# Windowed attention and top-1 experts: whole queries against masked keys in the first scores

## The reference

```python
q = (x @ wq.T + bq); k = (x @ wk.T + bk); v = (x @ wv.T + bv)      # by head, D = 16
loc = einsum('bnihd,bnjhd->bnihj', qw, kw) * D**-0.5               # in windows of 128
gsc = einsum('bihd,bjhd->bihj', q[:, ::32], k[:, ::32]) * D**-0.5  # global tokens, added
attn = softmax(scores, axis=-1)                                    # over all 2048 keys
x = layernorm(x + attn @ v @ wo.T + bo)
h = gelu((layernorm(x) * s_e + b_e) @ W1_e + b1_e); out = h @ W2_e + b2_e
x = layernorm(x + out of the expert argmax(x @ Wg.T))
```

## Time and profile before

| | us |
|---|---|
| median of 3 runs | 445.81 |
| lowest, highest | 444.01, 446.04 |
| profiled execution, span from first to last instruction | 442.8 |

### The profile page before, as it was taken

How to read it: one execution, slowest core, us unless ns; L and a number is a source line. 1 busy time by engine, 2 the same in 40 slices (tenths; PEclk the granted TensorE clock), 3 DMA queues, 4 the chain that set the end, 5 groups by cost and what they waited for, 6 DMA issues and landing times.

```text
span 442.8 us, 14658 instructions
## 1 busy us (share of the span) xinstructions
PE 405.3 (92%) x5747; PEld 339.8 (77%) x5747; DVE 326.1 (74%) x796; ACT 250.6 (57%) x523; POOL 220.4 (50%) x301
## 2 busy tenths in 40 slices
PE   5899799999999999999999899988798998999991
PEld 4758678888888888888888778756577887777891
DVE  6785687758757757757759888563668998899785
ACT  3424665675575575575576576676663555544421
POOL 4361343464464464464464566435733485477540
PEclk9999999999999999999999999999989999999997
DMA  8663740000000000000020000000000011011004
GB/s 240 186 199 111 240 137 4 27 25 0 24 24 0 24 24 0 24 24 0 24 72 4 25 2 3 3 1 2 0 2 2 1 49 47 0 47 49 34 15 143
DMA packets 21720, 20.34 MB, mean 46 GB/s; under 512 B 3133, under 2 KB 21682, under 8 KB 21682
## 3 DMA queue, kind: packets, MB, share of 16 engines
q1 hardware_dynamic: 16900, 15.07, 10.9%
q10 hardware_dynamic: 4782, 4.75, 3.3%
HBM read 15.41 MB, written 4.41 MB: 45 GB/s over the span
## 4 chain that ended last, share of the span: by engine, by line
PE 52%; DVE 26%; ACT 9%; issue 8%; DMA 3%; ACTq 1%; DVEq 0%; POOL 0%; POOLq 0%
DVE row_max_t L1154 10%; PE ps L1461 7%; PE ps L1737 7%; PE ps L1424 7%; PE ps L1562 5%; PE ps L1384 5%; PE ps L1415 4%; PE ps L1438 3%; PE ps L1444 3%; ACT probs L847 3%; DVE k_part L1013 2%; ACT boundsT_t L858 2%; PE ps L1406 2%; DMA rows<-in_L_attn_x_dram 2%; ACT k_part L713 2%
## 5 line engine op out<-in xcount | busy, mean ns | idle before, releaser
L847 ACT ACTIVATE probs<-ps 128x1024 f32<-128x1024 f32 x64 | 62.1, 1022 | 68.2 <-PE ps L1428 68.2
L1154 DVE TENSOR_REDUCE row_max_t<-ps 128x16 f32<-128x2048 f32 x31 | 70.9, 2287 | 3.7 <-PE ps L1415 3.6
L1737 PE MATMUL ps<-w_part,hm_part 128*128 128x256 f32 x384 | 53.8, 289 | 1.8 <-DVE hm_part L1332 1.8
L1415 PE MATMUL ps<-k_part,q_part 32*128 32x128 f32 x1584 | 51.5, 274 | 3.1 <-issue 1.5
L1415 PEld LDWEIGHTS ps<-k_part,q_part 32*128 32x128 f32 x1584 | 46.9, 186 | 9.2 <-issue 7.0
L1562 PE MATMUL ps<-xh_parts,w_part 128*128 128x512 f32 x192 | 53.8, 416 | 0.0
L557 POOL TENSOR_TENSOR q_part<-qf,q_part 128x512 fp32r<-128x512 f32 x32 | 41.0, 1281 | 25.7 <-ACT q_part L695 25.7
L599 POOL TENSOR_TENSOR attn_t<-num_t,rden_t 128x256 f32<-128x256 f32 x32 | 20.0, 624 | 64.7 <-DVE rden_t L1185 64.7
L1737 PEld LDWEIGHTS ps<-w_part,hm_part 128*128 128x128 f32 x384 | 48.2, 190 | 4.8 <-DVE hm_part L1332 2.4
L788 ACT ACTIVATE ffn_rows<-ps,b1s 128x512 f32<-128x512 f32 x32 | 22.0, 687 | 42.2 <-PE ps L1562 34.1
L1562 PEld LDWEIGHTS ps<-xh_parts,w_part 128*128 128x128 f32 x192 | 34.7, 194 | 6.5 <-issue 0.6
(11 more groups left out here) (234 smaller groups left out, 906.4 us busy)
## 6 DMA issues: line engine op xcount, KB each, us to landing
table<-rest_sums SPq DMA_DIRECT2D x4, 1088.0 KB, 6.1
xs<-in_L_attn_x_dram SPq DMA_DIRECT2D x16, 256.0 KB, 2.8
rows<-in_L_attn_x_dram ACTq DMA_DIRECT2D x4, 1024.0 KB, 8.1
out_dram<-yout SPq DMA_DIRECT2D x6, 512.0 KB, 2.9
w<-in_L_ffn_W_dram SPq DMA_DIRECT2D x2, 256.0 KB, 7.6
w<-in_L_ffn_W_dram SPq DMA_DIRECT2D x1, 512.0 KB, 4.2
out_dram<-yout SPq DMA_DIRECT2D x2, 256.0 KB, 2.6
out_dram<-yout ACTq DMA_DIRECT2D x2, 256.0 KB, 2.8
```

Of the source, the lines that this page charges most:

```text
L847: act.activation(probs[:, 2 * h:2 * h + 2, :], ps[:, 2 * h:2 * h + 2, :], ACT.Exp).then_inc(probs_ready, 1)
L1154: dve.tensor_reduce(row_max[:], ps_all, op=ALU.max, axis=AX.X).then_inc(max_ready, 1)
L1415: last = mm(ps[:, u, (2 * c + a) * P:(2 * c + a + 1) * P], q_part[x][quad(u), s, c, a, :], k_part[y][quad(u), s, c, :], start=(i == 0), st ...
L1737: mm(y, hm_part[a][:, 1 - p, f, c * P:(c + 1) * P], w2_part[b][:, f, :], start=(f == 0 and i == 0), stop=False)
```

## The change

The first scores now take the whole queries as weights, without mask or scale, and the keys masked and scaled, for both heads of a chunk side by side, as 256 moving columns. That is 24 products for a window where there were 48 of 128 columns. The turned scores are as before and still need masked queries. So:

- ACT writes the high part of the whole queries straight from PSUM (`q_whole[0]`, two instructions for two windows), DVE their low part (two instead of four). `qf` is gone.
- ACT's instruction moves from the odd step, behind its copy `aT`, to the even step, ahead of the exponentials.
- POOL makes all masked copies by `tensor_scalar`: 4 instructions for the keys of two windows (`mask_keys`, odd steps) and 4 for the queries (`mask_queries`, even steps), each over 128x512 elements; its two subtractions for two windows go. The masked keys lie in the first half of `xh_parts` (a single buffer for two windows, so they wait for the scores of the window before), the masked queries in `q_part` as before.
- First scores wait for `k_masked_ready`, turned scores for `q_masked_ready`.
- `take_high` of the first group moves on DVE from the end of step 30 to the end of step 31, ahead of `route`, since it writes where the masked keys lie.
- W1 is loaded at step 24, into the memory of `ysum[:, 1]`, ahead of W2 on SP's queue, and its three pieces of work on DVE move from steps 25, 26, 27 to 26, 27, 28.
- The global tokens keep the old form (`scores_of_globals`).

```diff
+        k_masked = [xh_parts[:, 0, i].rearrange("p c n -> p (c n)").rearrange("p (w c a n) -> p w c a n", w=2, c=KC, a=2)
+                    for i in range(2)]
...
+        q_whole = [sb(f"q_whole{i}", [P, SLOTS, KC, P], fp32r) for i in range(2)]
...
+        w1 = ysum[:, 1].rearrange("p t n -> p (t n)").rearrange("p (c e h) -> p c e h", c=KC, e=EXPERTS)
...
                     sp.wait_ge(rest_ready, NW // 2 + 1)
+                    for c in range(KC):
+                        sp.dma_start(w1[:, c, :, :], w1_dram[:, c * P:(c + 1) * P, :].rearrange("e p h -> p e h")).then_inc(ld_w1, 16)
                     sp.dma_start(w2[:], w2_dram.rearrange("(c e) h d -> (e h) c d", e=EPC)).then_inc(ld_w2, 16)
...
-            for c in range(KC):
-                sp.dma_start(w1[:, c, :, :], w1_dram[:, c * P:(c + 1) * P, :].rearrange("e p h -> p e h")).then_inc(ld_w1, 16)
             sp.dma_start(out_bias[:], bo_dram.rearrange("(a n) -> a n", a=1).broadcast_to([P, HID])).then_inc(ld_bo, 16)
...
-            def q_low(w, s):
-                need(pool, turned_scores_in_psum, w - 3)
-                pool.wait_ge(q_high_ready, w // 2 + 1)
-                pool.tensor_tensor(q_part[1][:, s], qf[:, s % 2], q_part[0][:, s].bitcast(fp32), ALU.subtract).then_inc(q_ready, 1)
+            def await_keys_high(w):
+                need(pool, scores_in_psum, w)
+                pool.wait_ge(k_high_ready, w // 2 + 1)
+            def await_keys_low(w):
+                pool.wait_ge(k_ready, w // 2 + 1)
+            def await_queries(w):
+                need(pool, turned_scores_in_psum, w - 2)
+                pool.wait_ge(q_ready, w // 2 + 1)
+            def mask_keys(i, s):
+                for a in range(2):
+                    pool.tensor_scalar(k_masked[i][:, :, :, a, :], k_part[i][:, s:s + 2].bitcast(fp32), q_scale[:, a, 0:1], None,
+                                       ALU.mult).then_inc(k_masked_ready, 1)
+            def mask_queries(i, s):
+                for a in range(2):
+                    pool.tensor_scalar(q_part[i][:, s:s + 2, :, a, :], q_whole[i][:, s:s + 2].bitcast(fp32), q_scale[:, a, 0:1], None,
+                                       ALU.mult).then_inc(q_masked_ready, 1)
...
             def step(t, s, steady=False):
...
+                keys_due = live(t + 1, steady) and p
+                queries_due = cur and p == 0 and (steady or t > 0)
+                if keys_due:
+                    await_keys_high(t + 1)
+                if queries_due:
+                    await_queries(t)
                 if pp:
...
-                if live(t + 1, steady) and (steady or t > 0):
-                    q_low(t + 1, (s + 1) % SLOTS)
+                if keys_due:
+                    mask_keys(0, (s + 1) % SLOTS)
+                if queries_due:
+                    mask_queries(0, s)
                 if cur:
...
+                    if keys_due:
+                        await_keys_low(t + 1)
                     need(pool, e_ready, t - 1)
...
+                if keys_due:
+                    mask_keys(1, (s + 1) % SLOTS)
+                if queries_due:
+                    mask_queries(1, s)
                 if older:
...
-            q_low(0, 0)
-            q_low(1, 1)
+            pool.wait_ge(dve_const, 4)
+            await_keys_high(0)
+            mask_keys(0, 0)
+            await_keys_low(0)
+            mask_keys(1, 0)
+            await_queries(0)
+            for i in range(2):
+                mask_queries(i, 0)
...
             def queries_of(w, s):
-                need(act, turned_scores_in_psum, w - 2)
-                act.wait_ge(qf_ready, w // 2 + 1)
-                copy(q_part[0][:, s:s + 2], qf[:]).then_inc(q_high_ready, 1)
+                need(act, turned_scores_in_psum, w - 3)
+                act.wait_ge(q_in_psum, w // 2 + 1)
+                for c in range(KC):
+                    last = act.activation(q_whole[0][:, s:s + 2, c, :], ps_xq[:, c * 2 * P:(c + 1) * 2 * P].rearrange("p (w n) -> p w n", w=2),
+                                          ACT.Identity, bias=bq_col[:, c:c + 1])
+                last.then_inc(q_high_ready, 1)
...
                     copy(aT[:].rearrange("p c n -> p (c n)"), ps_rao[:, 0:HID]).then_inc(aT_ready, 1)
-                if live(t + 1, steady) and p:
-                    queries_of(t + 1, (s + 1) % SLOTS)
...
+                if ahead and p == 0:
+                    queries_of(t + AHEAD, (s + AHEAD) % SLOTS)
                 if prev:
...
-            def queries_of(w):
-                need(dve, q_ready, w)
-                dve.wait_ge(q_in_psum, w // 2 + 1)
-                for k in range(2):
-                    for c in range(KC):
-                        last = dve.scalar_tensor_tensor(qf[:, k, c, :, :],
-                                                        ps_xq[:, (2 * c + k) * P:(2 * c + k + 1) * P].unsqueeze(1).broadcast_to([P, 2, P]),
-                                                        bq_col[:, c:c + 1], q_scale[:], ALU.add, ALU.mult)
-                last.then_inc(qf_ready, 1)
+            def queries_of(w, s):
+                dve.wait_ge(q_high_ready, w // 2 + 1)
+                for c in range(KC):
+                    last = dve.scalar_tensor_tensor(q_whole[1][:, s:s + 2, c, :], ps_xq[:, c * 2 * P:(c + 1) * 2 * P].rearrange("p (w n) -> p w n", w=2),
+                                                    bq_col[:, c:c + 1], q_whole[0][:, s:s + 2, c, :].bitcast(fp32), ALU.add, ALU.subtract)
+                last.then_inc(q_ready, 1)
...
-            dve.wait_ge(qg_ready, 1)
-            queries_of(0)
+            queries_of(0, 0)
             keys_of(0, 0)
...
-                if not steady and FACTORS_AT < t < FACTORS_AT + 4:
-                    split_first_layer(t - FACTORS_AT - 1)
+                if not steady and FACTORS_AT + 1 < t < FACTORS_AT + 5:
+                    split_first_layer(t - FACTORS_AT - 2)
                 if not steady and t in (2, 3):
                     stack_second_bias(t - 2)
-                if not steady and t == NW - 2:
+                if not steady and t == NW - 1:
                     for pair in range(2):
                         take_high(0, 0, pair)
-                if not steady and t == NW - 1:
                     for k in range(ROUTE_STEPS):
                         route(k, 0)
                     dve.wait_ge(b1_in_psum, 1)
...
                 if k == 0:
+                    dve.wait_ge(ld_w1, 16 * KC)
                     for c in range(KC):
...
             def scores(s):
                 for c in range(KC):
+                    for i, (x, y) in enumerate(SPLIT):
+                        for u in range(UNITS):
+                            last = mm(ps[:, u, 2 * c * P:(2 * c + 2) * P], q_whole[x][quad(u), s, c, :],
+                                      k_masked[y][quad(u), s % 2, c, :, :].rearrange("p a n -> p (a n)"),
+                                      start=(i == 0), stop=(i == 2), tile_position=(32 * u, 0))
+                return last
...
-                    pe.wait_ge(q_ready, t + 1)
-                    pe.wait_ge(k_ready, t // 2 + 1)
+                    pe.wait_ge(q_ready, t // 2 + 1)
+                    pe.wait_ge(k_masked_ready, 4 * (t // 2 + 1))
                     scores(s).then_inc(scores_in_psum, 1)
...
                 if prev:
                     pe.wait_ge(max_ready, upto(t + 1))
                     pe.wait_ge(boundsT_ready, t)
+                    pe.wait_ge(q_masked_ready, 4 * ((t - 1) // 2 + 1))
                     turned_scores((s + 3) % SLOTS).then_inc(turned_scores_in_psum, 1)
```

26 lines of the change are left out of this document (15 added, 11 removed).

## The result

The changed kernel takes 492.53 us (median of 4 runs, 489.29 to 493.96), the one before 444.91 (443.33 to 446.04): a ratio of 1.107, interval 1.101 to 1.113. I had forecast 443.7, so the miss is 49 us. The profiled execution took 489.29, the least of the four, with a span of 487.3 against 442.8.

The account below looks back on a forecast made before the run. Neither PE nor DVE alone was taken to set the pace; their chains alternate, even and odd steps. Loop -3.7, start +2.9, later steps -1.0, -0.6 and +0.3 sum to -2.1: 445.81 to 443.7 us, range 440.0 to 448.0.

Parts of the forecast that it names:

- rival 4: Loop, start and steps 25 and 26: POOL becomes the bound with masks at 1.28 each, 449.9 us; chance 0.09.
- Loop steps: Five passes of four steps: even steps 7.90, odd 8.38, a pass 32.56, saving 0.74 each, -3.7 us together.
- Start: Work before the loop and first steps: later dg and ACT's reordered exponentials against shorter scores, together +2.9 us.
- (b): Step 0: ACT's exponentials of the globals now stand behind the query copies, delaying PE's product of the rest, +3.1 us.
- (c): Steps 1 and 3: shorter scores give -0.6 in step 1, DVE's lighter queries -0.2 in step 3.
- (a): Start: DVE's low queries, waiting for ACT, go ahead of low keys and delay its dg, +0.6 us.
- Steps 24 to 32: After the loop: moved W1 work -1.0, step 30's shorter scores -0.6, step 31 with delayed route and onehot +0.3 us.
- Transfers: W1 and W2 loads from step 24: even one behind another they fit before use, 0 us.
- Rival 2: Start cheaper than counted (+0.5, not +2.9), with earlier transfers and DVE gaining more from lighter queries, 441.3 us; chance 0.2.
- Rival 1: Every step is shorter by the scores, DVE's chain having unseen slack: 19.5 less, 2.9 more, 429 us; chance 0.04.
- rival 5: First scores: moving columns alone set their cost, so they stay as dear as before, 447.6 us; chance 0.03.
- Rival 3: Every step: each new hand-over (ACT to DVE to POOL to PE) costs 0.1 a step over 28 steps, 446.5 us; chance 0.16.

Follow-up runs that it names:

- e3_forms: Changed kernel with the sixteen masks of a pass in eight forms side by side, seven of which don't compute masks; 456.7 us in one run.
- e6_two_input: Changed kernel, whole, each GpSimd mask made as a product with two inputs instead of a multiplication by a number of each partition; 463.9 us.
- e1_narrow: Changed kernel with every mask from step 3 on cut to 4 of each 128 columns (16 of 512); 451.2 us, 1.016 of before.
- e4_order: Changed kernel with ACT's step 0 query copies put back behind the globals' exponentials and the x_rest copy; 492.17 us in one run.
- e9_dg_first: Changed kernel, whole, with GpSimd's part of dg moved ahead of the first queries' masks before the loop; 490.8 us in one run.
- e5_take: Changed kernel with 16-column masks from step 3 on, masked keys in their own memory and take_high back in step 30; 445.6 us, 1.006 of before.
- e12: Changed kernel with all masks on GpSimd as two-input products, start orders mended, masked keys in own memory, take_high in step 30; 455.87 us in one run.
- e7: Changed kernel with ACT masking high parts, GpSimd low parts as two-input products, start orders mended, take_high in step 30; 438.63 us, 0.988 of before.

## Why the prediction was wrong, point by point

- **The price of a mask** is the step that failed: 0.66 taken, 1.28 as the far bound, 1.57 measured. I had the first condition right (late from 0.95) and in rival 4 the right mechanism, but at 1.28 for the price and with 32.0 for GpSimd's pass. What spoke for 0.66 was a select, which e3_forms shows to be no measure of a multiplication. The measured price puts its own sum at 11.5 + 16 x 1.57 = 36.6, and the pass took 38.2. With the price of rival 4 in fact built (e6_two_input) a pass took 33.9, and rival 4 gave 0.1 a step on 32.56, so 33.0: it named 0.95 as the point from which `attn` is late and charged no more for that. That GpSimd itself would decide from 1.25 isn't shown either, since at 1.28 it was busy for 31.4 of 34.2; what came through was `attn`. The row of the Trainium skill (GPSIMD Engine Reference, 4.1 Engine selection) on one-input work spoke for 0.66; the measurement speaks against it for a multiplication (1.57, against 1.28 with two inputs) and agrees for a copy (0.62).
- **Loop steps** with that price set aside: forecast 32.56, measured 32.36 (e1_narrow). Odd steps 8.32 (8.38 forecast), even ones 7.77 and 8.0 (7.90). This part was right.
- **Start**: forecast +2.9, measured +6.5 at T of step 1. (b) was right, 2.8 for 3.1 (e4_order). (c)'s shorter scores came, 0.6. The mis-sized term is (a), which looked at DVE alone. Before, the transposes of `dg` followed the product of the earlier trace rows that ends at 30.72 without a wait (PE starts them at 30.65); they now start at 34.80, 4.15 later, where I had 0.6. GpSimd's eight masks hold PE at two places ahead of them, at the first scores (2.37) and at GpSimd's part of `dg`, which starts at 32.83 (before at 26.62) and makes PE wait 1.19:

```profile
26.43 1.21 PE L1455 MATMUL ps<-xh_parts,q_whole 32*128 32x256 f32 x24 [2.37 <-POOL xh_parts L573]
...
34.80 1.97 PE L1646 MATMUL ps<-ident,dg 128*128 128x128 f32 x16 [1.19 <-POOL dg L677]
```

  Between the two the granted clock was 0.50 from 27 to 30, and a product took 2.07 where it had taken 1.13. In e9_dg_first the clock was 1.00 there and the transposes came 2.98 earlier, so more than the 1.19.
- **Steps 24 to 32**: forecast -1.3, and 64.53 against 66.15, so -1.6, once masks and `take_high` are taken out (e5_take). Of the term for steps 31 and 32 the delay by `take_high` was sized 0.5 and costs 3.1 in the last gap (less 0.4, by which the gap before it is shorter without `take_high`).
- **Transfers** at 0 stand: no wait for W1 or W2 is in the chain, and e5_take's end has their new place.
- **Rival 2**'s cheaper start did not come (+6.5), though a pass did gain more than forecast (0.95 for 0.74). **Rival 1** is refuted (32.4 a pass, not 30.8), **rival 5** too: 24 products of 256 columns take 0.98 where 48 of 128 took 1.56. **Rival 3** as well: the hand-overs are in e1_narrow, and its passes gain more than forecast.

The 38.2 of a pass can be split further. Over the five passes GpSimd was busy for 36.4 of each and idle for 1.8, and nearly all of its idle time is one wait, in odd steps, of `rest` for PE's first scores (total us, times, longest):

```profile
POOL rest_t L607 <- PE ps L1455: 8.3, 10, 1.1
```

This wait is new. The masked keys have a single buffer, so GpSimd may not fill it before the first scores have read it, and those come late behind `attn`, which GpSimd itself delays.

What stays open is how much of these 1.8 PE's lower clock makes: in the steps of 11.3 the clock is 0.85, in the even ones of 9.3 to 9.9 it is 1.00, and GpSimd is busy throughout in both. Nor was e12's 5.9 at the end followed by a run. Its trace has it in the gaps to T of steps 25, 27, 28 and 30 (1.3, 1.8, 1.7 and 1.0 longer than e7's), with PE waiting for `attn` 4.7 us in them where e7's PE waits 1.5.

## What to carry over

Price work on GpSimd by a row with the same operation, not the same number of inputs; where the trace has none, put the bound above the dearest row, and count what is queued behind the new work on its engine. Before giving an engine more, read its slack at each place where another waits for it (here 1.9 us between `e_arg` and `attn`), and put work there by that size. Here the shorter product paid only when its preparation went to idle time: with all masks on GpSimd it cost 11%, with half of them on ACT, and start and end mended, it gave 1.2%.

## What was unexpected of the hardware

- On GpSimd a TENSOR_SCALAR of 128 x 512 takes 1.57 us with a number of each partition and 1.49 with a constant, a TENSOR_TENSOR 1.28, a copy 0.62.
- DVE's own part of `dg`, two inputs from SBUF, takes 1.22 beside GpSimd's one-input masks in the changed kernel, and 4.40 beside the two-input masks of e12_all_pool:

```profile
L1098 DVE TENSOR_TENSOR dg<-dg,g_row 64x1024 f32<-64x1024 f32 x1 | 1.2, 1222 | 0.0
```

```profile
28.75 5.96 POOL L582 TENSOR_TENSOR q_part<-q_whole,q_scale 128x512 fp32r<-128x512 f32 x4
29.16 4.40 DVE L1103 TENSOR_TENSOR dg<-dg,g_row 64x1024 f32<-64x1024 f32 x1
...
33.62 2.53 PE L1652 MATMUL ps<-ident,dg 128*128 128x128 f32 x16 [2.66 <-DVE dg L1103]
```

  That is 3.2 us, and PE waits 2.66 for it. In e7_share, beside two two-input masks, it took 1.94, and PE's transposes came 2.64 earlier, which is most of the 3.41 by which e12's T of step 1 (46.71) lies behind e7's (43.30). The Trainium skill (SBUF — State Buffer, SBUF: two separate sides) says that a DVE instruction with two SBUF inputs and a GpSimd instruction that reads SBUF lock each other out of a shared pair of ports. The 4.40 agrees; the 1.22 beside one-input masks does not, since those read SBUF too.
- PE's wait for `attn` or `bounds` can have a second price. In the changed kernel, step by step, with the clock as last number but two:

```profile
133.21:141.54 8.33, 7.72 (x123) 6.67 (x122) 5.54 (x10) 5.64 (x13) 7.21 (x8) 1.00 0.00 0
141.54:151.40 9.86, 7.61 (x117) 6.42 (x117) 5.08 (x11) 5.04 (x11) 9.86 (x11) 1.00 0.08 27
151.40:160.00 8.60, 7.92 (x122) 6.66 (x121) 5.97 (x13) 5.74 (x13) 7.70 (x10) 1.00 0.00 0
160.00:171.33 11.33, 8.90 (x118) 7.40 (x118) 6.19 (x14) 5.04 (x11) 11.33 (x15) 0.85 0.08 23
```

  The second and the fourth step hold nearly the same products (117 and 118), which keep PE busy for 7.61 at full clock and 8.90 where part of the step was granted less. In the fourth the clock is 0.50 from 167 to 170, behind this wait:

```profile
165.93 0.41 PE L1721 MATMUL ps<-ident,attn_t 128*128 128x128 f32 x2 [2.43 <-POOL attn_t L635]
```

  In the second PE waited 1.93 at the same place and kept 1.00. But it also kept 1.00 behind the 2.82 of the start, so the length of one wait alone does not settle it.
